# A graph stage and an expert stage in one fp32 kernel: a placing step moved earlier, the last contraction cut in halves, filler matmuls in TensorE's pauses, and a weight request tied to TensorE's branch

## The chip, the cores and the metric

One NeuronCore of one Trainium2 chip runs the whole program. The metric is the device time of one execution in microseconds (us), lower being better. One execution was also taken by the hardware profiler; its own time and its span stand in the table further down. All times inside the trace count from the span's start.

## The reference

The input is x, 625 rows of 512 fp32 numbers. Two layers follow each other:

```python
# graph layer: 20000 edges, 64 paths, 16 segments of 32 columns
x1 = layernorm(x)[src].reshape(-1, 16, 32)
x2 = edge_attr.reshape(-1, 16, 32)
contrib = path_coeffs[None, :, None] * x1[:, i1, :] * x2[:, i2, :]
edge_out = zeros.at[:, i3, :].add(contrib)
x = x + zeros.at[dst].add(edge_out)          # dst is sorted
# expert layer on h = layernorm(x)
shared = sum over 2 shared experts of swiglu(h)
routed = sum over 64 experts of swiglu(h) * gate      # top 6 of 64 per row
x = x + shared + routed + h
```

Each expert, shared or routed, is three 512x512 fp32 matrices (gate, up, down), 1 MiB each. The 66 of them, 198 MiB, are read once.

## The kernel before, in words

**The graph layer.** The edges come in NG = 10 groups (the loop over `t` at lines 714 to 756), each with EC = 16 chunks of 128 edges (the first has 13). The 64 paths are worked in SUB = 8 steps `k` of HP = 8 paths; two steps make one of four parts. In a step VectorE multiplies, in `products` (L596 to L616), one 32-column segment of the gathered node rows with one of the edge rows, for all 16 chunks at a time: eight products of 128x512, the work on L611. TensorE then sums the 128 edges of each chunk into 32-row windows, in `contract` (L618 to L633, work on L630): 16 fp32 matmuls with 32 weight columns and 256 moving columns, four of them side by side in the four column strips of the array. The trace shows two records for one fp32 matmul, so 32 records. Behind the second step of a part come, for that part:

- `evict` on ScalarE (L640): the PSUM bank to SBUF;
- `turn` on TensorE (L647): four 128x128 transposes;
- `evict_turned` on ScalarE (L655);
- `select` on TensorE (L663): four matmuls that sort the paths into their segments.

Part q is contracted in steps 2q and 2q+1; its turn and its select are issued one step apart in the following two steps, so that they lie behind the contractions of the next part. After the four parts of a group `evict_sums` (ScalarE, L672) copies the sums, and `put` (TensorE, L679) multiplies them, for each of five blocks of 125 nodes, with `place`, a 128x625 matrix that puts the 32-row windows at their node rows. `place` is made by `place_rows`, two ScalarE operations over 625 columns (L594 and L596), issued at k = 7 behind that step's evict. The puts of group t-1 are issued in steps 2 to 6 of group t, one block each.

**The join.** For the last group there is no next one: its last turn, evict_turned, select, evict_sums and all five puts stand behind the loop in a row. VectorE adds each block to X (L685) and takes its statistics (L433), computes the second layer norm (L436 to L451), and TensorE transposes the normalised rows (L942), computes the router's logits (L925), and starts on the first shared expert (L875, `shared_up_part`). Later lines route the rows; the first gather of rows for an expert is on L1154, the first routed expert's gate and up matmuls are on L1262.

**A branch.** Between the last puts and the rest stands `with nc.If(nmax > 0)` around code for extra items (a window of nodes wider than 32 rows). For this input every engine jumps over it; the compare-and-branch instructions carry line L812. In TensorE's program this code is long (two items of eight contractions each).

**The requests for weights.** All weights are asked for by SyncE's queue, in program order, into a ring of four slots and one place for the shared expert. The ring's slots 0 and 1 are asked for within the last group. Then, behind the branch, stands what the change touches:

```python
sync.wait_ge(part_used, nparts)     # L818: all contractions are done
shw = [load_shared(0, *shared)]     # three transfers, issued on L309
load_expert(2, 2)                   # three transfers, L739 and L743
```

The memory that the first shared expert goes to is that of the products, which is why the contractions must be over. Next in SyncE's queue are the wait for the second layer norm, the store of its rows to `h_d` (L309), and expert 3. On TensorE the first things behind the branch are some semaphore increments (L855 to L861), `keep_clock(4)` (four matmuls whose result nobody reads, L916), and then

```python
pe.wait_ge(*shw[0])                 # all three matrices of the shared expert
```

ahead of the loop with the transposes of L942. From expert 4 on, a slot of the ring is asked for again when TensorE has finished with it.

Of the kernel before, what the change touches and what calls it, by code (L numbers as in the profile page):

```python
# [31 lines left out]
def gnn_moe(nc, x, src, dst, edge_attr, path_coeffs, path_indices, w_router,  # L32
# [7 lines left out]
    EXT = 32  # L40
# [223 lines left out]
    def sem(name):  # L264
        return nc.alloc_semaphore(name)
# [295 lines left out]
    nmax = nc.values_load(ntab[0:1, 0:1], min_val=0, max_val=MAXJ)  # L561

    part_used = sem("part_used")
    oh_ab, oh_ok = sem("oh_ab"), sem("oh_ok")
    pl_ab, place_ok = sem("pl_ab"), sem("place_ok")
    ev_ok, tp_ok, evt_ok, sel_ok, sum_ok = (sem(n) for n in ("ev_ok", "tp_ok", "evt_ok", "sel_ok", "sum_ok"))
# [31 lines left out]
    def products(t, s, edges, sources, chunks=EC):  # L598

        for k in range(SUB):  # L600
            rg = regs[k % 2]
            dve.load(rg, offs[0:1, 2 * HP * k:2 * HP * (k + 1)])  # L602
            if k == 0:
                dve.wait_ge(e_in[s], edges)
                dve.wait_ge(x_in[s], sources)
            if k > 1 or not at(t, 0):
                dve.wait_ge(part_used, SUB * t + k - 1)
            for p in range(HP):
                o1 = dve.snap(rg[2 * p], min_val=0, max_val=D - EXT)  # L609
                o2 = dve.snap(rg[2 * p + 1], min_val=0, max_val=D - EXT)  # L610
                ins = dve.tensor_tensor(pr[k % 2][:, 0:chunks, EXT * p:EXT * (p + 1)],  # L611
                                        xs[s][:, 0:chunks, ds(o1, EXT)], es[s][:, 0:chunks, ds(o2, EXT)], ALU.mult)
                if p == HP - 1:
                    ins.then_inc(part_ok, 1)
                if k <= EC // PER and (p % PER == PER - 1 or p == HP - 1):
                    dve.memset(opening[:, PER * k + p // PER:PER * k + p // PER + 1], 0.0)  # L616

    def contract(t, s, k, chunks=EC):  # L618

        h0 = HP * EXT * (k % 2)  # L620
        pe.wait_ge(part_ok, SUB * t + k + 1)
        if k == 0:
            pe.wait_ge(oh_ok, t + 1)
        if k % 2 == 0 and (k > 2 or not at(t, 0)):
            pe.wait_ge(evt_ok, PARTS * t + k // 2 - 1)
        for r in range(CW):
            for h in range(QW):
                if CW * h + r >= chunks:
                    continue
                ins = pe.matmul(edge_bank(k // 2)[WIN * h:WIN * (h + 1), h0:h0 + HP * EXT],  # L630
                                onehot[s][:, CW * h + r, :], pr[k % 2][:, CW * h + r, :], start=r == 0,
                                stop=r == min(CW, chunks - CW * h) - 1)
        ins.then_inc(part_used, 1)  # L633

    def evict(t, qq):

# [6 lines left out]
    def turn(t, qq):  # L643

        pe.wait_ge(ev_ok, PARTS * t + qq + 1)
        for f in range(FPP):
            ins = pe.transpose(edge_bank(qq)[:, P * f:P * (f + 1)], ev[:, P * f:P * (f + 1)], ident[:, :])  # L647
        ins.then_inc(tp_ok, 1)
# [8 lines left out]
    def select(t, qq):  # L657

        pe.wait_ge(evt_ok, PARTS * t + qq + 1)
        if qq == 0 and not at(t, 0):  # L660
            pe.wait_ge(sum_ok, t)
        for f in range(FPP):
            ins = pe.matmul(bank(BS)[:, P * f:P * (f + 1)], evT[:, P * f:P * (f + 1)], sel[:, qq, :],  # L663
                            start=qq == 0 and f == 0, stop=qq == PARTS - 1 and f == FPP - 1)
        ins.then_inc(sel_ok, 1)
# [28 lines left out]
    for t in range(NG):  # L694
        s = t % 2
        if 0 < t < NG - 1:
            load_edges(1 - s, SHORT + t * GE, SUB * t)
        if t < NG - 1:
            gather_sources(1 - s, idx, EC * (t + 1), SUB * t)
        chunks = EC if t else EC0  # L700
        products(t, s, 16 * QW * (t // 2 + 1), 16 * EC * (t // 2) + 16 * (EC if s else EC0), chunks)
        for k in range(SUB):
            contract(t, s, k, chunks)
            q = PARTS * t + k // 2 - 1
            if q >= 0 and k % 2 == 0:
                turn(q // PARTS, q % PARTS)
                evict_turned(q // PARTS, q % PARTS)
            if q >= 0 and k % 2 == 1:
                select(q // PARTS, q % PARTS)
            if k % 2 == 1:  # L710
                evict(t, k // 2)
            if t > 0 and k == 1:
                evict_sums(t - 1)
            if t > 0 and 2 <= k < 2 + NB:
                put(t - 1, range(k - 2, k - 1), start=t == 1)
            if t + 1 < NG and 2 <= k < 6:
                one_hots(t + 1, 1 - s, lambda c: wdst[:, EC * (t + 1) + c:EC * (t + 1) + c + 1],
                         CW * (k - 2), CW * (k - 1))
            if k == SUB - 1:
                place_rows(t, nrow[:, t:t + 1])  # L720
    turn(NG - 1, PARTS - 1)
    evict_turned(NG - 1, PARTS - 1)
    select(NG - 1, PARTS - 1)
    evict_sums(NG - 1)
    put(NG - 1, range(NB), stop=True)

    gu_in = [sem(f"gu_in{k}") for k in range(4)]
# [87 lines left out]
            pool.dma_start(none[s][k:k + 1, :], src[0:4].unsqueeze(0)).then_inc(y_out[s], 16)  # L815

    sync.wait_ge(part_used, nparts)  # L818
    shw = [load_shared(0, *shared)]
    load_expert(2, 2)  # L820

# [779 lines left out]
```

## Time and profile before

| what | value |
|---|---|
| time, median of 3 runs | 1060.63 us (1059.23, 1060.63, 1063.25) |
| profiled execution, own time | 1064.09 us |
| its span | 1062.9 us |
| mean granted TensorE clock | 0.974 |
| TensorE busy | 881.1 us (83%) |
| VectorE busy | 562.9 us (53%) |
| ScalarE busy | 226.3 us (21%) |
| bytes by DMA | 321.10 MB, mean 302 GB/s |

A share of busy time over the whole span mixes two stages with different limits, the graph layer up to about 430 us and the expert layer after it, so it says little about an edit at the seam. There the time is read from the chain of work and the timeline.

### The profile page before, as it was taken

To read this page: it belongs to the slowest core of one execution; us is meant where nothing else is said; L and a number is where in the kernel's file an instruction comes from. 1 tells how busy PE (TensorE), PEld (TensorE's weight loads), DVE (VectorE), ACT (ScalarE), POOL (GpSimd) and SP (SyncE) were. 2 spreads that over 40 slices of the span, in tenths; PEclk is the share of its full clock that TensorE was granted. 3 is DMA by queue.
4 is the path that set the end of the run, shared out by engine and by line. 5 is a ranking of instruction groups with operands and counts; after the bars stand their busy time and mean duration, and the time that the engine had idled before them with its cause. 6 is when DMAs were issued, how large, how long until landed. Compare 5 with 4: busy or idle time off the path is not lost.

```text
span 1062.9 us, 20671 instructions
## 1 busy us (share of the span) xinstructions
PE 881.1 (83%) x7145; PEld 477.0 (45%) x7146; DVE 562.9 (53%) x1321; ACT 226.3 (21%) x580; POOL 349.8 (33%) x390
## 2 busy tenths in 40 slices
PE   0267777677677677899999999999997999989988
PEld 0033333333334334485454544646444445445455
DVE  6499999999999999576211121121211221211116
ACT  1032232232233231241211111111210211211100
POOL 4654434434534520022322332333232232332120
PEclk9999899999999999999999999999998999999999
DMA  7857657657657654666999999999999999999928
GB/s 230 331 198 233 212 197 238 206 196 242 200 198 244 200 200 160 260 247 231 385 396 394 393 389 395 390 393 388 397 394 407 382 392 396 398 395 388 393 75 323
DMA packets 70374, 321.10 MB, mean 302 GB/s; under 512 B 12908, under 2 KB 13061, under 8 KB 48344
## 3 DMA queue, kind: packets, MB, share of 16 engines
q1 hardware_dynamic: 48050, 260.82, 64.5%
q0 software_dynamic: 21248, 56.55, 16.3%
q8 instruction: 94, 1.54, 0.6%
q10 hardware_dynamic: 934, 1.80, 0.6%
q14 instruction: 48, 0.39, 0.1%
HBM read 308.55 MB, written 13.62 MB: 303 GB/s over the span
## 4 chain that ended last, share of the span: by engine, by line
PE 57%; DVE 18%; issue 12%; DVEq 9%; DMA 2%; ACT 0%; ACTq 0%; another core or an unknown queue 0%
PE ps L1262 21%; DVE big L611 15%; PE ps L1320 11%; PE ps L875 7%; DVEq L609 4%; DVEq L602 4%; PE ps L1197 4%; PE ps L630 3%; PE ps L902 3%; PE ps L1294 2%; PE ps L1255 2%; DMA pair_d<-big 1%; PE ps L1314 1%; DVEq L611 1%; DMA big<-in_dst 1%
## 5 line engine op out<-in xcount | busy, mean ns | idle before, releaser
L611 DVE TENSOR_TENSOR big<-big 128x512 f32 (+1 forms) x640 | 385.0, 677 | 17.5 <-DMA big<-xn_d,idx 14.9
L630 PE MATMUL ps<-big,mixed 128*32 128x256 f32 x2512 | 171.8, 414 | 133.2 <-DVE big L611 120.7
L1262 PE MATMUL ps<-big 128*64 128x512 f32 x1024 | 237.0, 605 | 17.4 <-issue 16.4
L339 POOL DMA_INDIRECT big<-xn_d,idx x157 | 169.5, 1079 | 200.0 <-DVE big L611 144.7
L1154 POOL DMA_INDIRECT big<-h_d,idx x64 | 63.1, 986 | 361.6 <-issue 277.6
L630 PEld LDWEIGHTS ps<-big,mixed 128*32 128x32 f32 x2512 | 80.0, 116 | 227.5 <-DVE big L611 139.2
L1272 DVE TENSOR_TENSOR mixed<-big,ps 128x256 f32<-128x256 f32 x64 | 27.0, 422 | 268.9 <-ACT big L1269 268.5
L1262 PEld LDWEIGHTS ps<-big 128*64 128x64 f32 x1024 | 68.8, 138 | 142.4 <-issue 139.9
L1320 PE MATMUL ps<-big,mixed 128*64 128x256 f32 x1024 | 124.6, 385 | 0.1
L1223 POOL DMA_INDIRECT y_d<-big,sia x74 | 75.4, 1020 | 118.8 <-DVE big L1333 60.5
L1320 PEld LDWEIGHTS ps<-big,mixed 128*64 128x64 f32 x1024 | 67.9, 136 | 34.3 <-issue 2.9
L1332 DVE TENSOR_SCALAR big<-ps,gs 128x256 f32<-128x256 f32 x64 | 31.0, 484 | 97.2 <-PE ps L1320 85.4
L875 PE MATMUL ps<-big 128*128 128x125 f32 x640 | 76.8, 281 | 2.4 <-issue 2.4
L875 PEld LDWEIGHTS ps<-big 128*128 128x128 f32 x640 | 74.3, 195 | 6.4 <-issue 6.4
L1268 ACT ACTIVATE big<-ps 128x256 f32<-128x256 f32 x64 | 24.6, 384 | 239.3 <-PE ps L1262 236.6
L1299 ACT ACTIVATE mixed<-ps 128x384 f32<-128x384 f32 x64 | 31.4, 491 | 145.4 <-PE ps L1294 136.3
L1197 PEld LDWEIGHTS ps<-ident,big 64*128 64x128 f32 (+1 forms) x256 | 35.5, 210 | 50.3 <-issue 50.3
L640 ACT ACTIVATE mixed<-ps 128x512 f32<-128x512 f32 x40 | 23.9, 597 | 151.5 <-PE ps L630 110.5
L655 ACT ACTIVATE mixed<-ps 128x512 f32<-128x512 f32 x40 | 23.9, 597 | 149.0 <-PE ps L647 88.8
L679 PE MATMUL ps<-mixed 128*125 128x512 f32 x100 | 52.2, 612 | 0.7 <-ACT mixed L672 0.7
L663 PE MATMUL ps<-sel,mixed 128*128 128x128 f32 x320 | 48.0, 294 | 1.4 <-ACT mixed L655 1.2
L663 PEld LDWEIGHTS ps<-sel,mixed 128*128 128x128 f32 x320 | 40.2, 197 | 19.5 <-issue 18.0
(213 smaller groups left out, 653.0 us busy)
## 6 DMA issues: line engine op xcount, KB each, us to landing
big<-in_L_ffn_Wg SPq DMA_DIRECT2D x64, 1024.0 KB
big<-in_L_ffn_Wu SPq DMA_DIRECT2D x64, 1024.0 KB
big<-in_L_ffn_Wd SPq DMA_DIRECT2D x64, 1024.0 KB
big<-in_edge_attr SPq DMA_DIRECT2D x39, 1024.0 KB
big<-y_d SPq DMA_DIRECT2D x10, 768.0 KB, 11.8
big<-xn_d,idx POOLq DMA_INDIRECT x157
big<-in_L_ffn_sWg SPq DMA_DIRECT2D x2, 1024.0 KB, 5.1
big<-in_L_ffn_sWu SPq DMA_DIRECT2D x2, 1024.0 KB, 7.2
```

The source lines that it names most:

```text
L339: pool.indirect_dma_start(xs[s][:, c, :], None, xn_d[:, :], bass.IndirectOffsetOnAxis(ap=table[:, c0 + c:c0 + c + 1], axis=0)).then_inc(x_ ...
L602: dve.load(rg, offs[0:1, 2 * HP * k:2 * HP * (k + 1)])
L611: ins = dve.tensor_tensor(pr[k % 2][:, 0:chunks, EXT * p:EXT * (p + 1)], xs[s][:, 0:chunks, ds(o1, EXT)], es[s][:, 0:chunks, ds(o2, EXT)], ...
L630: ins = pe.matmul(edge_bank(k // 2)[WIN * h:WIN * (h + 1), h0:h0 + HP * EXT], onehot[s][:, CW * h + r, :], pr[k % 2][:, CW * h + r, :], st ...
L663: ins = pe.matmul(bank(BS)[:, P * f:P * (f + 1)], evT[:, P * f:P * (f + 1)], sel[:, qq, :], start=qq == 0 and f == 0, stop=qq == PARTS - 1 ...
L679: pe.matmul(bank(BM + b)[0:BP, :], place[:, BP * b:BP * (b + 1)], sums, start=start, stop=stop).then_inc(put_ok, 1)
L875: ins = pe.matmul(bank((og, ou)[w])[:, BP * j:BP * (j + 1)], shared[0][:, w, k, P * j:P * (j + 1)], hT[:, k, BP * b:BP * (b + 1)], start=k ...
L1154: pool.indirect_dma_start(xg[s][0:n], None, h_d[:, :], bass.IndirectOffsetOnAxis(ap=row, axis=0), bounds_check=N - 1, oob_is_err=False).th ...
L1197: ins = pe.transpose(bank(BT)[:, TB * k:TB * k + n], xg[s].rearrange("p (q k) -> p k q", k=KT)[0:n, k, :], ident[0:n, 0:n])
L1223: pool.indirect_dma_start(y_d.rearrange("r (h d) -> (r h) d", d=w), bass.IndirectOffsetOnAxis(ap=row_of(k), axis=0), yb[s][:, k * D // 2:k ...
L1262: ins = pe.matmul(bank(k2)[TA * h:TA * (h + 1), :].rearrange("p (w f) -> p w f", w=2), xgT[k2][:, k, 0:TA], gu[:, :, k, W * h:W * (h + 1)] ...
L1320: ins = pe.matmul(bank(BY)[TA * h:TA * (h + 1), 0:W], hTs[k2][:, o:o + TA], d[:, j, W * h:W * (h + 1)], start=j == 0, stop=j == FT - 1)
```

## The change

It has five pieces:

1. `place_rows` is issued at k = 6 instead of k = 7, in every group.
2. In the last group's last step `contract` is replaced by two calls of `contract_half`. Half 0 waits for the fourth of the step's eight products (new semaphore `half_ok`) and covers the left 128 of the 256 columns; half 1 waits for all eight. Between them stands the `select` of part 2, which before followed the whole contraction.
3. `stay_warm(3)` ahead of the last turn, `stay_warm(4)` ahead of the last select, `stay_warm(2)` ahead of the last puts: fp32 matmuls of the identity with itself, 128x128, into a PSUM bank that is free.
4. A TensorE nop behind the branch increments a new semaphore `past_extra`.
5. SyncE waits for it before it asks for the first shared expert and expert 2.

```diff
     def products(t, s, edges, sources, chunks=EC):
+                if p == HP // 2 - 1 and k == SUB - 1 and at(t, NG - 1):
+                    ins.then_inc(half_ok, 1)
...
+    def contract_half(t, s, half):
+        k, w = SUB - 1, HP // 2 * EXT
+        if half == 0:
+            pe.wait_ge(half_ok, 1)
+        else:
+            pe.wait_ge(part_ok, SUB * t + k + 1)
+        for r in range(CW):
+            for h in range(QW):
+                ins = pe.matmul(edge_bank(k // 2)[WIN * h:WIN * (h + 1), HP * EXT + w * half:HP * EXT + w * (half + 1)],
+                                onehot[s][:, CW * h + r, :], pr[k % 2][:, CW * h + r, w * half:w * (half + 1)],
+                                start=r == 0, stop=r == CW - 1)
+        if half == 1:
+            ins.then_inc(part_used, 1)
+
+    def stay_warm(n):
+        for _ in range(n):
+            pe.matmul(edge_bank(PARTS - 2)[:, 0:P], ident[:, :], ident[:, :], start=True, stop=True)
...
         for k in range(SUB):
-            contract(t, s, k, chunks)
+            last = t == NG - 1 and k == SUB - 1
+            if last:
+                contract_half(t, s, 0)
+            else:
+                contract(t, s, k, chunks)
...
             if q >= 0 and k % 2 == 1:
                 select(q // PARTS, q % PARTS)
+            if last:
+                contract_half(t, s, 1)
...
-            if k == SUB - 1:
+            if k == SUB - 2:
                 place_rows(t, nrow[:, t:t + 1])
+    stay_warm(3)
     turn(NG - 1, PARTS - 1)
     evict_turned(NG - 1, PARTS - 1)
+    stay_warm(4)
     select(NG - 1, PARTS - 1)
     evict_sums(NG - 1)
+    stay_warm(2)
     put(NG - 1, range(NB), stop=True)
...
+    past_extra = sem("past_extra")
+    pe.nop().then_inc(past_extra, 1)
     sync.wait_ge(part_used, nparts)
+    sync.wait_ge(past_extra, 1)
     shw = [load_shared(0, *shared)]
     load_expert(2, 2)
```

## Rows read from the trace of the kernel before

**Rows 1.** Busy time by stretch: PE, PEld, DVE, ACT, POOL, granted clock, DMA share, GB/s.
```profile
421.00:431.00 10.00, 7.61 (x92) 3.75 (x80) 8.13 (x14) 1.19 (x2) 0.00 (x0) 1.00 0.01 2
...
436.00:440.00 4.00, 4.00 (x6) 1.53 (x6) 2.22 (x4) 0.00 (x0) 0.00 (x0) 0.57 1.01 386
```

**Rows 2.** Chain that ended last, 421 to 447 us: start, length, what.
```profile
423.65 5.49 DVE big L611 x9
...
429.19 1.98 PE ps L630 x32
...
431.79 0.72 ACT mixed L594
...
435.72 3.38 PE ps L679 x4
...
443.80 0.71 DVE bn L433
```

**Rows 3.** Timeline, 419 to 450 us: start, length, instruction, count, idle before it and releaser.
```profile
426.73 1.02 PE L679 MATMUL ps<-mixed 128*125 128x512 f32 x2
...
431.05 1.16 PE L663 MATMUL ps<-sel,mixed 128*128 128x128 f32 x8
432.05 0.60 PE L647 MATMUL ps<-ident,mixed 128*128 128x128 f32 x4
433.88 1.16 PE L663 MATMUL ps<-sel,mixed 128*128 128x128 f32 x8 [1.23 <-ACT mixed L655]
435.72 6.25 PE L679 MATMUL ps<-mixed 128*125 128x512 f32 x10 [0.69 <-ACT mixed L672]
443.25 3.67 PE L916 MATMUL ps<-big 128*128 128x512 f32 x8 [1.27 <-issue]
447.24 1.20 PE L942 MATMUL ps<-ident,big 125*128 125x125 f32 x8 [0.33 <-DVE big L451]
...
433.25 0.58 ACT L655 ACTIVATE mixed<-ps 128x512 f32<-128x512 f32 x1
...
437.42 0.69 DVE L685 TENSOR_TENSOR X<-X,ps 125x512 f32<-125x512 f32 x1 [8.29 <-PE ps L679]
```

**Rows 4.** The same timeline at the end of the kernel: a contraction of 128 columns.
```profile
1024.35 1.08 PE L1314 MATMUL ps<-big,mixed 128*32 128x128 f32 x32 [0.84 <-ACT mixed L1299]
```

**Rows 5.** Branches by line: engine, count, ns min/median/max, first and last start.
```profile
L812 SPq COMPARE_BRANCH  x1: 45/45/45, 415.1 to 415.1; - x1
...
L812 PEldq COMPARE_BRANCH  x1: 6701/6701/6701, 435.8 to 435.8; - x1
...
L1500 PEldq COMPARE_BRANCH  x1: 3720/3720/3720, 1025.9 to 1025.9; - x1
```

**Rows 6.** Busy time by stretch while TensorE takes the later branch (columns as rows 1).
```profile
1026.00:1029.00 3.00, 1.31 (x14) 0.58 (x8) 0.74 (x2) 0.00 (x0) 0.26 (x1) 1.00 0.15 46
```

**Rows 7.** SyncE's queue: its issues, and the landing of the shared expert's three transfers.
```profile
431.18 0.35 SPq L309 DMA_DIRECT2D big<-in_L_ffn_sWg  x1
...
432.05 0.43 SPq L309 DMA_DIRECT2D big<-in_L_ffn_sWd  x1
...
448.95 0.91 SPq L309 DMA_DIRECT2D h_d<-big  x2
...
DMA to landing us min/median/max: 5.1/7.2/10.7
```

**Rows 8.** After a long pause of TensorE (columns as rows 1), and the matmuls behind it.
```profile
801.00:808.00 7.00, 0.20 (x2) 0.01 (x1) 0.57 (x2) 0.49 (x1) 2.00 (x2) 0.77 1.02 396
809.00:811.00 2.00, 2.00 (x6) 0.47 (x4) 0.00 (x0) 0.00 (x0) 0.00 (x0) 0.50 1.05 432
...
808.69 3.81 PE L1262 MATMUL ps<-big 128*64 128x512 f32 x10 [7.48 <-issue]
```

**Rows 9.** The first gather of rows, and a stretch after it (columns as rows 1).
```profile
461.54 1.02 POOL L1154 DMA_INDIRECT big<-h_d,idx  x1 [80.09 <-DVE one L1018]
...
500.00:600.00 100.00, 98.78 (x635) 49.73 (x636) 19.95 (x57) 19.37 (x50) 33.24 (x39) 1.00 1.02 388
```

More of the change, by code:

```diff
@@ L563, in gnn_moe @@
     part_used = sem("part_used")
+    half_ok = sem("half_ok")
     oh_ab, oh_ok = sem("oh_ab"), sem("oh_ok")
```

## The prediction

> **What bounds the kernel at the seam.** Busy time by stretch comes first. Up to 430 us VectorE is the busy engine and the DMA engines carry next to nothing; from 436 to 440 us the DMA engines are full and TensorE's granted clock is 0.57, the lower level (1.2 GHz) for most of it [rows 1]. The chain of waits then says what ends last: VectorE's products to 429.14 us, the last contraction (1.98 us), a ScalarE copy of 0.6, then placing on ScalarE from 431.79, the slow puts, and VectorE's adds and statistics [rows 2]. The timeline shows the joints: the last turn starts at 432.05, behind a select; its result waits for ScalarE until 433.25 although the turn is over at 432.65, since placing stands in between; the puts start at 435.72, the first add at 437.42, the transposes of the normalised rows at 447.24 [rows 3]. Behind the seam everything hangs on that 447.24, so I work out when it comes after the change. Further on the DMA engines are full (share 1.02 from 500 to 600 us) [rows 9]; their backlog starts with slots that TensorE frees, so a shift of TensorE at the seam passes through to the end one to one.
>
> **Last contraction in halves.** The products of the last step end at 429.14, eight of about 0.61 us (5.49 for nine [rows 2]), so the fourth ends near 426.7. TensorE is free of the put of 426.73 at about 427.6: two 512-column records of 0.43. Half 0 has the shape of the later contraction with 32 records of 128 columns, 1.08 us [rows 4]; half of 1.98 would be 0.99, and with the weight loads unhidden it could be 1.45, the most I allow. I take 1.08: half 0 to 428.7, the select (8 records, 1.00 to the next start [rows 3]) to 429.7, half 1 with its fill to 430.9. Before, the contraction ended at 431.17. Gain 0.3 (bounds: a loss of 0.4, a gain of 0.5).
>
> **Placing.** Its two operations move to ScalarE's pause behind evict_turned of part 2. Its wait there is for the put of step 6, over by 427.75 [rows 3]; it is done by 429.4, and the evict queued behind it needs ScalarE at 430.9. Cost nothing; if the cover went, at most 1.5. In the other nine groups ScalarE is idle there and VectorE sets the pace: nothing.
>
> **Identity matmuls.** One is two records at the select's rate, 0.125 each. Evict ends at 431.5, three identity products end with it: the turn starts at 431.55 and is over at 432.2. ScalarE copies at once, to 432.8. Four products take 1.0 from 432.05 and end at 433.05, so the select starts 0.2 later than it could, is over at 434.2, the sums at 434.85. Two products take 0.5 of a 0.65 pause. The puts start at 434.9 instead of 435.72: gain 0.8, placing 0.6 of it.
>
> **The clock in the puts.** The first two puts took 3.38 us as four records [rows 2], 0.85 each, twice the 0.43 of the later ones; ahead of them TensorE had paused 1.23 and 0.69 us [rows 3]. With these pauses filled I expect the upper level. The first add then starts 0.97 after the puts, at 435.9, not 1.70 after; a wait of some 0.35 for the second block goes too. From the first add to the end of the last statistics it was 7.1 (437.42 to 444.5 [rows 2, 3]); without that wait it is 6.7, so they end at 442.6, and the transposes could start at 445.3: **1.9 us gained**, if nothing else holds them.
>
> **The weight request.** This is the piece that decides. TensorE's branch is recorded from 435.77 for 6.70 us [rows 5], while six requests of 1 MiB each, issued from 431.18 [rows 7], fill the DMA engines. The only other long branch of TensorE took 3.72 us with a DMA share of 0.15 [rows 5, 6]. The Trainium skill ("Runtime: NRT & Kernel Launch", Instruction fetch mechanics) says that a taken branch whose target lies outside the window forces a DMA fetch of the target page; both rows fit. So the new order shortens the branch by about 3.0. But it starts only at 434.95 (the puts are queued by then), ends at 438.65, and SyncE asks at about 438.75 instead of 431.18: **7.6 us later**. The third transfer landed 10.7 after its issue at 432.05 [rows 7], so all three were there at 442.75, 11.6 after the first issue and 4.5 us ahead of the transposes. Now they are there at 438.75 + 11.6 = **450.3**. TensorE waits for all three ahead of the transposes, so these start at 450.35, not at 445.3: 3.1 us later than before. Bounds: a branch as short as other engines' and a landing quicker by 1 us give 446, a loss of 6.7 for the branch gives 453.4.
>
> **The clock after that wait.** keep_clock ends at about 442.6 (puts to 439.2, eight records of 0.43 behind them), so TensorE pauses 7.7 us. After a pause of 7.48 us at 801 to 808 us the clock was at 0.50 up to 811, nearly 3 us after the matmuls of 808.69 began [rows 8]. Router and transposes run back to back on TensorE there; 2.9 us at half speed cost at most 1.45. I take 1.2 (bounds 0 and 2.5). The Trainium skill ("TensorE: Matmul & The Clock Gate", Why this matters for your kernels) warns against long idle gaps between matmul bursts; by that rule the change moves the slow stretch from the puts to the router and does not remove it.
>
> **What else is queued behind SyncE's new wait.** Expert 2, needed much later; and the store of the normalised rows, issued at 448.95 before, now near 447. Six transfers kept the engines busy some 17 us from the first issue, to about 456 now; the store's 1.25 MB then have until the first gather, 461.54 before [rows 9] and near 465.8 now. I cost it at nothing; if its cover goes, 1 to 3 us.
>
> **Sum.** 450.35 - 447.24 = +3.1, clock +1.2: **+4.3 us**. On the profiled execution's own 1064.09 that is 1068.4; this execution stood 3.5 above the median of the runs, so against 1060.63 I say **1065**.
>
> **Rivals.**
> 1. *The weights come in time*: the branch takes well under 1 us, as SyncE's does (45 ns [rows 5]), or the three matrices land faster with the DMA engines to themselves. Request at 435.6, landing at 446 to 447: between 0 and 1.3 gained, the full 1.9 at best, 1058.7 to 1060.6. For it speaks that no idle-DMA branch of this size is in the trace with nothing beside it; against it the 3.72 us row. Chance 0.15.
> 2. *The branch is not shortened* (the side of slower): its 6.70 us are its own, whatever the DMA engines carry. Request at 441.8, landing at 453.4, transposes 6.1 later, with the clock +7.3: 1068. It decides once the branch takes over 4.7 us. Against it stands the 3.72 us row, though that was another target. Chance 0.13. The Trainium skill ("DMA: Bandwidth & Descriptors", Queues, rings and completion order) speaks for it: each DMA engine goes round its queues packet by packet, so weights in flight would cost a fetch little more than a packet's wait.
> 3. *The store is late*: it queues behind six transfers and the first gather waits for it, +4.3 and 1 to 3 more: 1066 to 1068. It decides if the store lands after 466. Chance 0.1.
> 4. *The wait is there but costs less*, since the slow clock does not come or TensorE's branch starts early: +1 to +3, 1062 to 1064. Chance 0.17.
>
> The forecast keeps 0.45, spread over 1063 to 1067.
>
> **Numbers.** About 0.5% (5.3 us) is what a measurement of this kernel can tell from no change. Faster by that needs 1055.3 or less, beyond any case here: 0.04 for what I don't see. Slower by that starts at 1065.9: rivals 2 and 3, and the upper third of the forecast: 0.36. The rest, 0.60, is within. The range goes from rival 1 to beyond rival 2: 1059.3 to 1069.5.
>
> **What would show it.** Right: SyncE's first L309 issue behind 431 at 438 to 439.5; TensorE's branch record near 3.7; puts at 434.9 with 0.43 per record; the last statistics near 442.6; a TensorE pause of about 7 us behind L916, ended by a DMA on the shared expert; transposes near 450.3 with a granted clock near 0.5. Wrong: transposes before 447.2 (then the request was no later than the path allows), half 0 ending after 429.2, or slow puts in spite of the filler.

## The result and the profile after

The changed kernel takes 1070.85 us (median of 6 runs, 1067.96 to 1077.23) against 1061.14 of the kernel before: ratio 1.0099, 95% interval 1.0076 to 1.0123, so it is **slower by 9.7 us between the medians, about 1%**. The forecast was 1065, range 1059.3 to 1069.5. The profiled execution is the slowest of the six, with 1077.23 us of its own, so its trace shows more than the median loss.

Times in two traces are best compared from one event. I take the end of the last product on VectorE: 429.13 us before, 425.74 after (the products are the same but for one semaphore increment; this point lies between 425 and 430 us in most traces and between 438 and 443 in those of e9 to e12). "At +x" below means x us behind it. Before: puts at +6.6, first add +8.3, transposes +18.1, first routed expert's gate and up matmuls +38.1.

TensorE's timeline of the changed kernel, from the first half to the router (start, length, instruction, idle before it and releaser):

```profile
424.29 1.08 PE L647 MATMUL ps<-big,mixed 128*32 128x128 f32 x32
425.30 1.16 PE L686 MATMUL ps<-sel,mixed 128*128 128x128 f32 x8
426.38 1.08 PE L647 MATMUL ps<-big,mixed 128*32 128x128 f32 x32
...
428.68 1.06 PE L656 MATMUL ps<-ident 128*128 128x128 f32 x8
...
431.37 4.56 PE L702 MATMUL ps<-mixed 128*125 128x512 f32 x10 [0.24 <-ACT mixed L695]
438.86 5.28 PE L951 MATMUL ps<-big 128*128 128x512 f32 x8 [2.93 <-issue]
448.38 1.66 PE L977 MATMUL ps<-ident,big 125*128 125x125 f32 x8 [4.25 <-DMA big<-in_L_ffn_sWd]
449.89 1.94 PE L960 MATMUL ps<-wr,big 128*125 128x64 f32 x8
451.62 1.04 PE L977 MATMUL ps<-ident,big 125*128 125x125 f32 x4
...
475.50 3.65 PE L1297 MATMUL ps<-big 128*64 128x512 f32 x16
```

The first pieces of the change do what they were to do: the puts start at +5.6, take 4.56 us instead of 6.25 [rows 3], and the pauses ahead of them are gone. Then come two things that [rows 3] did not have. TensorE waits 4.25 us for the shared expert's third matrix (448.38), and what follows is slow: four transpose records take 1.04 from start to end instead of 0.68, the first routed expert comes at 475.50, +49.8 instead of +38.1. The rows of TensorE's sequencer and of SyncE's queue say where the wait came from (durations in ns as min/median/max, then the start in us; the last line gives the times from issue to landing of the shared expert's requests, the first of which is the line above it):

```profile
L844 PEldq COMPARE_BRANCH  x1: 3650/3650/3650, 431.4 to 431.4; - x1
...
L851 PEldq EVENT_SEMAPHORE  x1: 51/51/51, 435.1 to 435.1; - x1
...
L890 PEldq EVENT_SEMAPHORE  x1: 51/51/51, 438.1 to 438.1; - x1
...
L309 SPq DMA_DIRECT2D big<-in_L_ffn_sWg x1: 345/345/345, 435.3 to 435.3; - x1
...
DMA to landing us min/median/max: 5.2/8.5/11.1
```

The branch takes 3.65 us instead of 6.70 [rows 5]. The request goes out at 435.3, at +9.5 instead of +2.1. And there is a pause that nobody had foreseen: TensorE's sequencer runs one instruction behind the branch (L851, the new nop) and the next one (L890) 3.0 us later. The stretches behind the stall, with the clock (columns as rows 1):

```profile
449.00:454.00 5.00, 5.00 (x26) 4.76 (x25) 0.96 (x7) 2.00 (x4) 0.00 (x0) 0.50 1.01 403
454.00:460.00 6.00, 6.00 (x32) 6.00 (x31) 2.49 (x19) 1.85 (x5) 0.00 (x0) 0.50 1.04 418
460.00:466.00 6.00, 6.00 (x24) 5.40 (x24) 3.17 (x18) 5.21 (x17) 0.00 (x0) 0.50 0.62 258
467.00:470.00 3.00, 3.00 (x33) 3.00 (x32) 2.51 (x7) 1.09 (x3) 0.14 (x1) 1.00 0.02 5
```

For comparison, two lines of the kernel before, from the same transposes and router:

```profile
449.56 0.68 PE L942 MATMUL ps<-ident,big 125*128 125x125 f32 x4
...
454.00:461.00 7.00, 6.92 (x59) 6.50 (x57) 6.23 (x30) 6.27 (x18) 0.00 (x0) 1.00 1.00 389
```

The granted clock is at its lower level for all of the router, 17 us, although TensorE is busy without a gap. So of the 11.6 us at the first routed expert 4.5 are the stall (+22.6 against +18.1) and the other 7.1 the slow stretch behind it.

The seam is not the whole difference between the two traces. From the first routed expert to the end of the span it is 600.5 us in the changed kernel and 595.6 before, another 4.9 us. With the products ending 3.4 us earlier that adds up: 4.5 + 7.1 + 4.9 - 3.4 = 13.1, which is 1077.23 less 1064.09, the own times of the two profiled executions. Where the 4.9 come from is taken up under "Where the branch lands".

### The profile page after: what moved, and what is told of

Read it like the earlier page. It is cut to its first block, busy times and chain, and to the rows that moved or that the text cites. A ratio compares the mean times of both kernels' runs of the same rounds, so it can differ in the third digit from the quotient of the medians.

```text
span 1076.0 us, 20773 instructions
## 1 busy us (share of the span) xinstructions
PE 889.3 (83%) x7195; PEld 486.1 (45%) x7196; DVE 561.9 (52%) x1321; ACT 228.4 (21%) x580; POOL 350.4 (33%) x390
## 3 DMA queue, kind: packets, MB, share of 16 engines
q0 software_dynamic: 21248, 56.55, 16.1%
q8 instruction: 96, 1.57, 0.6%
## 4 chain that ended last, share of the span: by engine, by line
PE 61%; DVE 15%; issue 9%; DVEq 8%; DMA 4%; POOL 1%; SPq 0%; PEld 0%; ACT 0%; POOLq 0%; PEldq 0%
PE ps L1297 20%; DVE big L612 12%; PE ps L1355 10%; PE ps L633 9%; PE ps L910 7%; DVEq L610 4%; PE ps L1232 3%; DVEq L603 3%; PE ps L937 3%; DMA big<-in_L_ffn_Wu 2%; PE ps L1329 2%; PE ps L1290 2%; POOL big L339 1%; DMA big<-in_L_ffn_sWd 1%; DVEq L612 1%
## 5 line engine op out<-in xcount | busy, mean ns | idle before, releaser
L633 PE MATMUL ps<-big,mixed 128*32 128x256 f32 x2480 | 167.0, 408 | 131.6 <-DVE big L612 131.6
L1297 PE MATMUL ps<-big 128*64 128x512 f32 x1024 | 239.7, 611 | 18.9 <-issue 16.6
L1307 DVE TENSOR_TENSOR mixed<-big,ps 128x256 f32<-128x256 f32 x64 | 26.9, 421 | 272.2 <-ACT big L1304 271.8
L678 ACT ACTIVATE mixed<-ps 128x512 f32<-128x512 f32 x40 | 23.9, 597 | 154.3 <-PE ps L670 154.3
L663 ACT ACTIVATE mixed<-ps 128x512 f32<-128x512 f32 x40 | 23.9, 597 | 133.3 <-PE ps L633 131.9
## 6 DMA issues: line engine op xcount, KB each, us to landing
big<-in_L_ffn_Wg SPq DMA_DIRECT2D x64, 1024.0 KB, 16.4
big<-in_L_ffn_sWg SPq DMA_DIRECT2D x2, 1024.0 KB, 10.2
```

The lines of the kernel that those rows point to most:

```text
L1297: ins = pe.matmul(bank(k2)[TA * h:TA * (h + 1), :].rearrange("p (w f) -> p w f", w=2), xgT[k2][:, k, 0:TA], gu[:, :, k, W * h:W * (h + 1)] ...
```

## The experiments

All ratios are to the kernel before, run beside each version on the same chip; the positions are those of one trace each. "Late request" is SyncE's wait for the branch. "Skipped" instructions stand inside the code that TensorE's branch jumps over; they never run and only move the code behind. The "place" says by how many instructions, modulo 256, TensorE's code of the expert stage lies further than before; it is counted from the edits, four instructions for one fp32 matmul (two weight loads and two matmul records). The first instruction behind the branch that both kernels have (L855 before, L890 in the changed kernel, right behind the new nop) has the same place, except where matmuls were added behind it: there it is at 101 in e4, 224 in e13 and 0 in e11 and e12.

| kernel | late request | pieces 1 to 3 | place | transposes | first routed expert | median us | ratio (95%) |
|---|---|---|---|---|---|---|---|
| before | no | no | 0 | +18.1 | +38.1 | 1061.14 | |
| changed | yes | yes | 101 | +22.6 | +49.8 | 1070.85 | 1.0099 (1.0076 to 1.0123) |
| e1 | yes | no | 1 | +21.8 | +48.1 | 1070.73 | 1.0086 (1.0071 to 1.0102) |
| e2 | no | yes | 101 | +23.9 | +43.8 | 1069.97 | 1.0075 (1.0061 to 1.0090) |
| e3 | yes, wait at use | yes | 101 | +18.7 | +42.7 | 1074.60 | 1.0118 (1.0101 to 1.0134) |
| e4 | yes, stall filled | yes | 129 | +24.8 | +44.6 | 1068.60 | 1.0063 (1.0045 to 1.0080) |
| e5 | no | yes | 0 | +16.4 | +36.3 | 1065.14 | 0.9994 (0.9982 to 1.0006) |
| e6 | yes | yes | 0 | +20.8 | +47.1 | 1073.30 | 1.0069 (1.0056 to 1.0082) |
| e7 | no | no | 101 | +17.2 | +37.1 | 1068.34 | 1.0028 (1.0015 to 1.0042) |
| e8 | yes, wait at use | yes | 0 | +16.1 | +42.3 | 1071.27 | 1.0055 (1.0042 to 1.0068) |
| e9 | no | no | 100 | +25.2 | +45.1 | 1091.40 | 1.0134 (1.0106 to 1.0162) |
| e10 | no | no | 180 | +17.3 | +37.3 | 1078.68 | 1.0007 (0.9991 to 1.0024) |
| e11 | expert 2 only | yes | 8 | +19.6 | +39.5 | 1076.68 | 0.9991 (0.9970 to 1.0013) |
| e12 | yes, filler behind stall | yes | 12 | +26.9 | +46.9 | 1082.49 | 1.0048 (1.0031 to 1.0064) |
| e13 | yes, stall filled | yes | 0 | +21.1 | +41.8 | 1067.10 | 1.0050 (1.0031 to 1.0069) |
| e14 | as e6 | yes | 0 | +21.6 | +48.5 | 1069.30 | 1.0062 (1.0041 to 1.0083) |
| e15 | no | yes | 180 | +16.2 | +36.2 | 1061.47 | 1.0001 (0.9987 to 1.0016) |

The kernel before took 1061.87 us beside e1 to e4, 1065.15 beside e5 to e8, 1077.52 beside e9 to e12 and 1060.89 beside e13 to e15. So medians of different groups are compared by their ratios, not as they stand.

### The late request alone, and the rest without it

```diff
 e1, against the kernel before
+    past_extra = sem("past_extra")
+    pe.nop().then_inc(past_extra, 1)
     sync.wait_ge(part_used, nparts)
+    sync.wait_ge(past_extra, 1)
 e2, against the changed kernel
-    sync.wait_ge(past_extra, 1)
```

> The kernel before with the new semaphore behind TensorE's branch and SyncE's wait for it, and nothing else of the change. Theory A (the late request is the whole loss, through a stall of TensorE on the shared expert and a clock that then stays low through the router): first L309 issue behind the branch at about 439.5 if the products end at 429, all three matrices there 12 to 13 us later, transposes 4.5 to 6 us later than before, granted clock 0.5 for ten us or more behind them, first routed expert 10 to 13 us later; time +9 to +13 us. Rival B (half of the loss comes from the other pieces): at most +6 us.

> The changed kernel without SyncE's wait for the new semaphore; the earlier placing, the halves and the filler stay. Theory A: no stall on the shared expert, the clock stays at its upper level through the router, the transposes 15.9 to 16.5 us after the last product instead of 18.1; time 1.5 to 2.5 us below the kernel before. Rival B: the filler or the halves cost something of their own, the time is no better than before or some us above it. Rival C: the branch of TensorE takes 6.5 us or more again and now holds the transposes: no gain.

e1 gave nearly the whole loss: transposes at +21.8, clock 0.5 for the first 15.5 us behind them (it had fallen 1.5 us earlier, in the stall), first routed expert 9.9 later, +8.9 us. By itself this would be theory A. But e2 fits none of the three theories: with the weights landed at +14.1 it started its transposes at +23.9 and lost 8.1 us. The branch took 6.59 us, as rival C says, but it was over at +12.3 and did not hold the transposes. Its rows, branch first, then the matmuls of keep_clock (L950) and the transposes (L976):

```profile
L844 PEldq COMPARE_BRANCH  x1: 6590/6590/6590, 431.5 to 431.5; - x1
...
L851 PEldq EVENT_SEMAPHORE  x1: 51/51/51, 438.2 to 438.2; - x1
...
L889 PEldq EVENT_SEMAPHORE  x1: 51/51/51, 443.6 to 443.6; - x1
...
444.35 5.54 PE L950 MATMUL ps<-big 128*128 128x512 f32 x8 [8.36 <-issue]
449.73 1.11 PE L976 MATMUL ps<-ident,big 125*128 125x125 f32 x8
```

The pause behind the first instruction is there again, 5.5 us now that the weights are in flight, 3.0 in the changed kernel. keep_clock starts after it, part of it at the lower clock. In the changed kernel the same pause costs nothing at the transposes, since the stall on the shared expert ends later still; taking the late request away brought it to light. In e1, whose code moved by one instruction, there is none.

### Moving the wait to where the data is used; filling the stall

```diff
 e3, against the changed kernel
-    pe.wait_ge(*shw[0])          # ahead of the transposes
     ...
     route(NB - 1)
+    pe.wait_ge(*shw[0])
     shared_up_part(0, BEU, 1, 0, 7)
 e4, against the changed kernel
-    keep_clock(4)
+    keep_clock(11)
```

> The changed kernel, late request included, with TensorE's wait for the shared expert moved from ahead of the transposes to ahead of the first matmul that reads it. Theory A: the transposes start about 16 us after the last product, near 442 to 443 in a trace like the one of after; TensorE then pauses on the shared expert behind the router until about 22.5 us after the last product; as the logits are there early, the first routed expert moves by some 4 us or less against the kernel before; the clock stays up in the router. Time between 2 below and 4 above the kernel before. Rival B (stall costs nothing, clock falls for another reason): clock 0.5 through the router as in after, time +6 or more.

> The changed kernel with 11 instead of 4 of the matmuls of 512 columns between the branch and the wait for the shared expert, so that TensorE is busy in the stall; nothing is taken from the stall itself. Theory A (of the 11.7 us at the first routed expert some 4.5 are the stall and 7 the low clock behind it): transposes start as late as in after or up to 2 later, router at clock 1.0, first routed expert 4.5 to 6.5 later than before; time 5 to 7 us below that of the changed kernel. Rival B (the low clock does not set the end, the shift is the stall's and the DMA's): time within 2 us of the changed kernel.

e3 took the stall away (transposes at +18.7, held by keep_clock behind the second pause) and was yet the slower kernel. Its first gather went out at +32.9, 11 us earlier than in the changed kernel, while the DMA engines were still full (share 1.03 from 445 to 463 us) with the late requests, the store and expert 3, and TensorE waited for it just before the first routed expert, which then ran at the lower clock:

```profile
465.95 0.92 PE L1232 MATMUL ps<-ident,big 96*128 96x96 f32 x4 [2.81 <-DMA big<-h_d,idx]
...
468.73 6.41 PE L1297 MATMUL ps<-big 128*64 128x512 f32 x16
```

6.41 instead of 3.65 for the same 16 records. The delay had moved to the next user of the same DMA engines, and the clock fell in the pause it made. That does not account for all of the 12.7 us: the first routed expert starts only 4.5 later than before, and from there to the end it is 605.6 us instead of 595.6. The place of the code has a part in that: e8, the same with the code at place 0, has 595.3 there and loses 6.1 us. e4 left the stall and kept TensorE busy in it: its transposes came 2.1 later than in the changed kernel, its first routed expert 5.2 earlier. So the low clock is a cost of its own. In the time e4 gained less than its expectation said (5 to 7 us below the changed kernel): its ratio is 1.0063 against 1.0099, about 3.8 us, and its later code also lies at another place.

### Where the branch lands

e5, e6 and e8 are e2, the changed kernel and e3 with 155 skipped instructions (101 + 155 = 256); e7, e9 and e10 are the kernel before with 101, 100 and 180:

```diff
+    padding = sem("padding")
     with nc.If(nmax > 0):
+        for _ in range(155):
+            pe.nop().then_inc(padding, 1)
         dve.wait_ge(put_ok, NB * NG)
```

> e2 (the change without SyncE's new wait) with 155 semaphore instructions of TensorE added inside the code that the branch jumps over; they are never executed and only move all of TensorE's code behind them, which the change had moved by 101 instructions, to a distance of 256 from where it stood before (64 B each, 16384 B, the size of one fetch packet). Theory D (placement of the branch's target in a fetched block): no second pause behind the nop after the branch, so keep_clock starts at about 12.5 us after the last product instead of 18.5, the transposes 15.6 to 17 after it instead of 23.9; first routed expert 1 to 2.5 earlier than in the kernel before; time 1 to 3 us below before, 9 to 11 below e2. Rival E (the pause of e2 is the weights' traffic, wherever the target lies): as e2, +8 us.

> The changed kernel with the same 155 skipped instructions. Theory D: TensorE's first instructions behind the branch follow at once, keep_clock directly behind the puts; the stall on the shared expert stays (transposes 21 to 22.6 us after the last product) and so does the low clock behind it; first routed expert 9 to 11 later than before; time within 1.5 us of e1 (only the late request), 0 to 2 below the changed kernel. Rival E: equal to the changed kernel.

> The kernel before, unchanged in all that it executes, with 101 skipped instructions of TensorE inside the code that the branch jumps over, so that its later code lies as in the changed kernel. Theory D: behind the branch (about 6.7 us) a second pause of 5 to 6 us after one to three instructions, keep_clock 5 us later than before, transposes 5 to 6.5 us later, time +6 to +9 us. Rival E (the executed instructions of the change matter, not the placement): no difference from the kernel before, within 1 us.

> e3 (late request, TensorE's wait for the shared expert at its first use) with the 155 skipped instructions. Theory D: transposes 15.6 to 16.5 us after the last product at clock 1.0; TensorE pauses behind the router until the shared expert is there, 21.5 after the last product; the first gather is issued 1 to 3 us earlier than before but lands late, as in e3 (7 us instead of 3), while the late requests and expert 3's still run; first routed expert 1 to 4 later than before; time between 0 and +5 us, well below e3's +12.7. Rival E: as e3.

In e5 the instruction behind the nop follows at once, keep_clock starts at 442.42 and the transposes at +16.4:

```profile
L854 PEldq EVENT_SEMAPHORE  x1: 51/51/51, 441.5 to 441.5; - x1
...
L892 PEldq EVENT_SEMAPHORE  x1: 51/51/51, 441.6 to 441.6; - x1
...
442.42 3.67 PE L953 MATMUL ps<-big 128*128 128x512 f32 x8 [2.73 <-issue]
445.93 1.11 PE L979 MATMUL ps<-ident,big 125*128 125x125 f32 x8
```

The executed instructions are those of e2, and the 8.1 us of loss are gone; the 1 to 3 us below the kernel before that the expectation asked for did not come (0.9994). e6 loses 0.69% instead of the changed kernel's 0.99%, with the first routed expert 9.0 later. e8 starts its transposes at +16.1, but the clock falls behind them; its first routed expert comes 4.1 later (forecast 1 to 4) and it loses 6.1 us (forecast 0 to 5). e7 showed no pause and spoke against theory D as I had put it; but the changed kernel had run exactly one instruction behind its branch, so a border at 101 means that a target at 101 is the first of its block. e9 tested it, one instruction less:

> The kernel before with 100 skipped instructions, one less than in e7. In the changed kernel the nop behind the branch ran at once and the next instruction only after a second pause; in e7 (101) there was none. Theory D (a fetched block ends there): at 100 the branch's target is the last instruction of its block, so one instruction runs, then a pause of 4.5 to 6 us while the weights are in flight; keep_clock 5 us later and partly at the lower clock, transposes 22.5 to 24.5 us after the last product; time +6 to +9 us. Rival E (e7 shows that shifting does nothing at the branch): as e7, transposes at 17 to 18, +2 to +4 us.

> The kernel before with 180 skipped instructions: the target lies 80 behind a block's start. Theory F (the position of the code costs microseconds in the expert stage too, as e7's +3 us suggest, which had no pause at the branch): nothing changes up to the first expert, but the time differs from before by 1 to 5 us either way. Rival G (e7's +3 us come from something else): within 1 us of before.

```profile
L858 PEldq EVENT_SEMAPHORE  x1: 51/51/51, 454.6 to 454.6; - x1
...
L862 PEldq EVENT_SEMAPHORE  x1: 51/51/51, 460.3 to 460.3; - x1
...
460.86 6.25 PE L919 MATMUL ps<-big 128*128 128x512 f32 x8 [7.99 <-issue]
466.94 1.11 PE L945 MATMUL ps<-ident,big 125*128 125x125 f32 x8
```

One instruction, then 5.7 us. With nothing changed in what it executes, the kernel before loses 1.34% by 100 skipped instructions, more than the 6 to 9 us of the expectation: 6.9 us at the first routed expert, and another 7.6 behind it (603.2 us to the end of the span instead of 595.6). The Trainium skill ("Runtime: NRT & Kernel Launch", Instruction fetch mechanics) says that instructions come in blocks of 16 KiB, 256 instructions, by DMA, one block ahead of execution. The runs fit this, with a border found between 100 and 101 and none at 180 or 256. The same section of the Trainium skill counts a crossing as mostly hidden; here it cost 3.0 and 5.5 us.

The DMA records show the fetch itself. In the changed kernel, whose branch goes from 431.43 to 435.08, one packet of kind "instruction" and 16 KiB moves from 432.43 to 433.72, and the next only from 435.83 to 436.88, 0.75 us behind the branch's end. In the kernel before (branch from 435.78) the first moves from 440.07 to 441.06. The lines of that queue (packets, MB, share) for the windows 432.4 to 433.7 and 435.8 to 436.9 in the changed kernel, and for 457.7 to 458.8 in e9, within the pause behind its one instruction; from 433.8 to 435.7 in the changed kernel and from 453.2 to 457.6 in e9 the queue moved nothing:

```profile
q8 instruction: 1, 0.02, 6.2%
...
q8 instruction: 1, 0.02, 5.9%
```

```profile
q8 instruction: 1, 0.02, 6.2%
```

All 17 traces have this order. The packet starts 1.0 us after the branch does where the weights are asked for behind it, and 3.5 to 4.3 us after it with weights in flight; it moves for 1.0 to 1.5 us, and the branch ends 1.4 to 1.5 us behind its end. So what the weights cost the branch is the wait ahead of the packet. The next block's packet starts behind the branch's end in every trace, 0.7 us behind it with the late request and 3.2 to 3.5 us with the early one (1.3 in e11). Where the branch lands early in its block no pause shows (before, e1, e5 to e8, e10 to e15); where it lands on the last instruction of its block, TensorE waits for that packet. That queue 8 is TensorE's is read from these times.

There is a second effect of place. From the first routed expert to the end of the span it is 599.1 to 603.2 us in the changed kernel, e2, e7 and e9 (places 100 and 101; e3, at the lower clock there, has 605.6) and 595.2 to 598.4 in all others. Branches of the experts' down step, 64 of them (min/median/max ns), in before, changed, e7, e9 and e10, in this order:

```profile
L1310 PEldq COMPARE_BRANCH  x64: 65/208/348, 481.2 to 1024.2; - x64
```

```profile
L1345 PEldq COMPARE_BRANCH  x64: 65/322/3163, 489.4 to 1036.9; - x64
```

```profile
L1313 PEldq COMPARE_BRANCH  x64: 65/320/2938, 480.0 to 1028.0; - x64
```

```profile
L1313 PEldq COMPARE_BRANCH  x64: 65/320/2443, 500.7 to 1048.3; - x64
```

```profile
L1313 PEldq COMPARE_BRANCH  x64: 65/208/428, 493.8 to 1039.2; - x64
```

At places 100 and 101 (with e2 and e3) the longest take 2.4 to 3.2 us, at place 129 (e4) 0.7, elsewhere 0.4 at most. e7, which pays nothing at the first branch (its first routed expert is 1.0 earlier than before), still loses 0.28%; e10 at 180 doesn't, so of its two theories only the one that expected less than 1 us of difference is near (+0.07%, within the interval). That these branches are the reason is an inference: the place was varied, the branches alone were not. And they show only in part as idle TensorE. In the changed kernel the matmuls behind them waited 1.2 us in all (sum, times, longest):

```profile
PE ps L1355 <- issue: 1.2, 2, 1.0
```

In e7 it is 1.0. How the rest of the 4.9 and 5.8 us at this place comes about stays open.

### The clock behind the stall

```diff
 e12, against e6
     pe.wait_ge(*shw[0])
+    keep_clock(3)
 e13, against the changed kernel (123 skipped instructions)
-    keep_clock(4)
+    keep_clock(12)
```

> e6 (the change, code in its old position) with three more matmuls of 512 columns behind the wait for the shared expert, ahead of the transposes. Theory C (the low clock behind the stall lasts because of what TensorE does next: transposes and the router do not bring it back, long matmuls do): the six records start at 0.85 us each, the clock is up within some 3.5 us, transposes 3 to 5 us later than in e6, but the router then runs at the upper level, 1.33 instead of 2.4 per block, and the first routed expert is 1 to 4 earlier than in e6. Rival: the clock stays low for 14 to 20 us after such a pause whatever runs: transposes 5 later and everything 4 to 5 later than e6.

> The change with 12 instead of 4 matmuls in keep_clock, so that they last until the shared expert is there, and 123 skipped instructions, so that the code behind lies where it lay in the kernel before (as in e6). Theory (stall and clock are two costs of similar size): transposes 21 to 22.5 us after the last product, hardly later than in e6; granted clock at the upper level through the router; first routed expert 3 to 5 later than before instead of 9 to 10; time 4 to 7 us below e6 in the same call. Rival (the stall alone sets the loss): within 2 us of e6.

> e6 once more, on the chip of this call, as the measure for e13: +7 to +8.5 us over the kernel before, transposes 20.8 to 22 us after the last product, clock 0.5 for over 10 us behind them.

Three stretches of e14 and of e13 from the router on (columns as rows 1):

```profile
446.00:452.00 6.00, 5.21 (x25) 4.98 (x26) 0.96 (x7) 1.99 (x4) 0.00 (x0) 0.50 1.00 410
452.00:458.00 6.00, 6.00 (x32) 6.00 (x31) 1.92 (x14) 1.84 (x5) 0.00 (x0) 0.50 1.05 417
458.00:462.00 4.00, 4.00 (x20) 4.00 (x20) 3.00 (x19) 2.54 (x14) 0.00 (x0) 0.50 0.99 416
```

```profile
446.00:452.00 6.00, 5.53 (x44) 4.99 (x44) 1.92 (x14) 2.86 (x7) 0.00 (x0) 1.00 1.01 413
452.00:458.00 6.00, 5.92 (x47) 5.50 (x47) 4.81 (x31) 4.76 (x18) 0.00 (x0) 1.00 1.04 408
458.00:462.00 4.00, 4.00 (x42) 4.00 (x42) 3.25 (x8) 3.31 (x6) 1.02 (x1) 1.00 1.00 421
```

The same wait ends at +21.6 and +21.1; the first routed expert comes at +48.5 and +41.8. So in these traces 3.5 or so are the stall, 6 to 7 the clock.

In the medians the two kernels are only 2.2 us apart, within their intervals: the 4 to 7 us of the expectation did not come, and its rival (within 2 us) is about as near. So 7 us is what the clock cost in a trace, and what it costs a typical execution is not settled. The runs of e14 spread from 1066 to 1072 us, with mean clocks from 0.977 to 0.968, the lowest clock not always with the longest run, those of e13 with clocks of 0.974 and above. The means of these are 0.972 and 0.978; over 1068 us that makes, as an estimate, about 13 us more at the lower level in a run of e14 than in one of e13; in the traced one the stretch was 20.5 us.

In e12 three long matmuls ran behind the stall; the clock was back at 465.38, 5.3 us after TensorE had resumed and as they ended, and the router was fast:

```profile
460.06 5.47 PE L954 MATMUL ps<-big 128*128 128x512 f32 x6 [7.89 <-DMA big<-in_L_ffn_sWd]
465.34 1.12 PE L981 MATMUL ps<-ident,big 125*128 125x125 f32 x8
```

Its first routed expert is at +46.9, 0.2 earlier than in e6 (the expectation said 1 to 4, with the clock back after 3.5 us): what the filler costs the router gives back. The rival, 14 to 20 us at the lower level whatever runs, predicted 4 to 5 later and fell; the low stretch was 10.2 us.

### Half of the traffic, and another place for the gain

```diff
 e11, against e5
     sync.wait_ge(part_used, nparts)
     shw = [load_shared(0, *shared)]
+    sync.wait_ge(past_extra, 1)
     load_expert(2, 2)
-    keep_clock(4)
+    keep_clock(6)
```

> e5 (early request, code in its old position) with SyncE's wait for the branch moved between the shared expert's three requests and those for expert 2, and six instead of four matmuls in keep_clock. Theory: half the traffic competes with the fetch, so the branch takes 4.5 to 6 us instead of 6.2; the shared expert lands earlier than 13.5 after the last product (11 to 13); the transposes start 15.6 to 16.4 after it with the clock up; first routed expert 1.9 to 2.5 earlier than before; time 0 to 2 us below before. Rival: the gain at the first expert is given back in the expert stage as in e5, time within 1 us of before.

> e2 with 79 skipped instructions, so that the later code lies 180 instructions behind its place in the kernel before, as in e10, which took as long as before. Theory (halves, filler and earlier placing gain about 1.9 us that hold): transposes 16 to 16.6 us after the last product, no pause behind the branch, time 1 to 2.5 us below before. Rival (given back in the expert stage): time within 1 us of before, as e5.

e11's branch took 6.08 us against 6.25 in e5: three requests in flight delay the fetch as much as six; the branch ended at 450.5, before the third of them had landed at 452.0. The shorter branch of the expectation (4.5 to 6 us) and the earlier landing (11 to 13 after the last product; it was 13.2) did not come. The two added matmuls, 7.08 us for the twelve records, then sit on the path (+19.6). Its time is that of before. e5 and e15 have the first routed expert 1.9 us earlier than in the trace of before, and both take as long as before within their intervals, as the rival of e15 says. Against e7 and e10, the unchanged kernel in traces without the slow puts (+37.1 and +37.3), they are only 0.8 to 1.0 us earlier, too little for these intervals. No version here is measurably faster than the kernel before.

## Why the prediction was wrong, step by step

- **Direction and deciding piece: right.** The late request costs more than the other pieces gain, by a stall on the shared expert ahead of the transposes. e1 shows it alone.
- **Halves, placing, filler: right to 0.1 us in the positions.** Puts at +5.6 (forecast +5.8), first add +6.8 (+6.8), last statistics' end at +13.5 (+13.5). But the slow puts, which the filler was to remove, are in part chance: of the five traces without filler before and e1 have them (6.25 us), e7, e9 and e10 do not (4.56 us, with the first add at +7.75 and not +8.3). So about half of the 1.9 us was the luck of the trace of before, and no gain shows in the time (e5, e15).
- **The branch: right.** 3.65 us, forecast 3.7. Rival 2 (not shortened) fell, and with it what it took from the Trainium skill ("DMA: Bandwidth & Descriptors", Queues, rings and completion order): with weights in flight the fetch's packet started 2.5 to 3.3 us later, not a packet's wait.
- **The landing: undersized.** From the first request to the last landing it was 13.1 us, forecast 11.6. The stall made +4.5, not +3.1. SyncE's second request took 1.57 us to issue instead of 0.43, but 1.43 and 1.47 in e1 and e6 too, where the whole was 11.5 and 11.4; there the third transfer landed 9.6 and 9.5 us behind its issue, here 11.1. Why this one was slower stays open.
- **The clock behind the stall: the step that failed.** The term "clock +1.2" of the sum (bounds 0 and 2.5) measured 7.1 us in the trace. I took a pause in the expert stage as the model, behind which 512-column matmuls ran and the clock was back after some 3 us. Behind this pause transposes and the router's matmuls ran, and it stayed low for 17 us. e13, e4 and e12 show in their traces that cost apart from the stall; in the medians it is smaller (2.2 us between e14 and e13, about 3.8 between the changed kernel and e4), so its size in a typical execution stays open.
- **Missing altogether: the place of the code.** The change adds 100 of TensorE's instructions ahead of the branch's target and the nop at it, so the nop became the last instruction of its block. That made the pause of 3.0 us behind it (hidden in the changed kernel, 8 us of loss in e2) and goes with the 4.9 us behind the first routed expert, a term that the sum did not have. At the old place the changed kernel lost 0.69 and 0.62% (e6, e14) instead of 0.99%; the intervals of e14 and the changed kernel overlap, so I put about 2 to 3 us on it, without proof for the size. The pause is also why keep_clock came late and part of it ran at the lower clock (8 records in 5.28 us), and why TensorE's wait for the shared expert was 4.25 us and not the 7.7 of the forecast; in e6 it was 7.06.
- **The store and first gather: as costed**, at nothing in the changed kernel; in e3 the gather did become the next wait.
- **A shift at the seam passes to the end: only roughly.** On one chip the first routed expert comes at +36.3, +42.3 and +47.1 in e5, e8 and e6, and the rest to the end of the span takes 598.4, 595.3 and 596.1 us.

## What to carry to other kernels

A request that is made later to spare one waiter must be followed to every other waiter on it, with the landing time of the requests as they were, and a stall on TensorE is to be costed with what runs behind it: if that is short matmuls and transposes, the low clock can last several times longer (17 us here) than behind a pause that ends in long ones (3 us in the trace of before, 5.3 in e12). Before two versions of a program with far branches are compared, shift the code behind the branch by some skipped instructions, in both; a difference of a per cent (1.34% in e9) can come from where the target falls, and then belongs to no edit.

## What the runs showed of the hardware

- One hundred instructions that are never executed cost 13.9 us (e9), 101 cost 3.2 (e7), 180 nothing measurable (e10).
- A far branch of TensorE took 3.4 to 3.8 us where the weights were asked for behind it and 6.0 to 6.7 with weights in flight, in every trace; the difference lies ahead of the instruction packet, which starts 1.0 or 3.5 to 4.3 us after the branch does. The pause for the following block was 3.0 to 3.5 and 5.5 to 5.7 us.
- The clock stayed at its lower level through 17 us of back-to-back transposes and router matmuls (15.5 us in e1, 15.7 in e6, 16.7 in e14), yet the same work at the upper level did not bring it down in before, e5 or e13. It rose as three matmuls of 512 columns ended in e12. What in the work decides this was not tried apart.
- keep_clock can come too early: in e8 the branch was over soon, keep_clock ended 2.3 us ahead of the transposes, and 2 us into them the clock fell, for 13.7 us.
